# Four-layer sequence kernel: attention output transfers on GpSimd's queue, the first batch's split parts stored once, the first fills issued from two queues

## The reference

```python
c6 = silu(c) @ Wc + bc
sh_msa, sc_msa, g_msa, sh_mlp, sc_mlp, g_mlp = split(c6, 6)
xm = modulate(layernorm(x), sh_msa, sc_msa)
q, k, v = heads(xm @ Wq + bq) / 16, heads(xm @ Wk + bk), heads(xm @ Wv + bv)
w = softmax(q @ k.T, axis=-1)
x = x + g_msa * (merge(w @ v) @ Wo + bo)
x = x + g_mlp * (gelu(modulate(layernorm(x), sh_mlp, sc_mlp) @ W1 + b1) @ W2 + b2)
```

## Time and profile before

| | us |
|---|---|
| median of 3 runs (lowest, highest) | 965.06 (964.97, 965.78) |
| the profiled execution | 965.65 |
| its span in the trace | 963.8 |
| PE busy in the span | 899.0 (93%) |
| DVE, ACT, POOL busy | 585.8, 521.3, 417.0 |

### The profile page before, as it was taken

How to read it: one execution, slowest core, us unless ns; L and a number is a source line. 1 busy time by engine, 2 the same in 40 slices (tenths; PEclk the granted TensorE clock), 3 DMA queues, 4 the chain that set the end, 5 groups by cost and what they waited for, 6 DMA issues and landing times.

```text
span 963.8 us, 14588 instructions
## 1 busy us (share of the span) xinstructions
PE 899.0 (93%) x5256; PEld 539.6 (56%) x5256; DVE 585.8 (61%) x914; ACT 521.3 (54%) x952; POOL 417.0 (43%) x556
## 2 busy tenths in 40 slices
PE   5779999899899989998999998999999999999997
PEld 3444344334336778787788675343443433588874
DVE  4657877588975375556433178678778886234423
ACT  2118777476766445345265432567677776744431
POOL 4333152242648546347634434762441015575331
PEclk9979999799999999999999999999999999999999
DMA  7466656455310230014025125565464421100001
GB/s 221 118 192 219 206 153 172 140 138 159 92 46 33 81 129 1 23 56 158 1 93 200 12 79 158 160 190 168 131 196 134 112 80 47 46 13 1 23 22 44
DMA packets 67151, 102.33 MB, mean 106 GB/s; under 512 B 16540, under 2 KB 27880, under 8 KB 66696
## 3 DMA queue, kind: packets, MB, share of 16 engines
q1 hardware_dynamic: 63876, 97.50, 33.6%
q10 hardware_dynamic: 3204, 3.90, 1.3%
HBM read 64.65 MB, written 36.07 MB: 104 GB/s over the span
## 4 chain that ended last, share of the span: by engine, by line
PE 72%; DVE 8%; ACT 5%; issue 4%; DMA 4%; POOL 3%; SPq 3%; ACTq 0%; DVEq 0%; POOLq 0%
PE PS L1048 12%; PE PS L666 12%; PE PS L636 12%; PE PS L1030 11%; PE PS L593 6%; PE PS L584 6%; PE PS L645 3%; ACT PH L727 3%; DVE U L823 2%; PE PS L430 2%; DMA d_parts<-UR 2%; PE PS L604 2%; PE PS L1163 1%; PE PS L1151 1%; POOL PHR L1095 1%
## 5 line engine op out<-in xcount | busy, mean ns | idle before, releaser
L823 DVE TENSOR_REDUCE U<-PS 128x2 f32<-128x1024 f32 x256 | 308.4, 1219 | 70.9 <-PE PS L645 69.7
L727 ACT ACTIVATE PH<-PS 128x512 f32<-128x512 f32 x512 | 277.6, 598 | 103.3 <-PE PS L636 99.9
L636 PE MATMUL PS<-UR 50*128 50x512 f32 x512 | 197.1, 456 | 11.2 <-ACT PH L727 5.9
L645 PE MATMUL PS<-UR 48*128 48x512 f32 x512 | 193.8, 473 | 12.9 <-DMA UR<-d_parts 6.6
L1095 POOL TENSOR_TENSOR PHR<-PH,PHR 128x512 fp32r<-128x512 f32 x96 | 128.8, 1346 | 118.2 <-ACT PHR L1085 118.2
L636 PEld LDWEIGHTS PS<-UR 50*128 50x128 f32 x512 | 83.0, 188 | 167.8 <-ACT PH L727 107.1
L1048 PE MATMUL PS<-UR,PHR 128*128 128x256 f32 x768 | 159.9, 291 | 4.8 <-POOL PHR L1095 3.6
L666 PE MATMUL PS<-PH,U 128*32 128x512 f32 x1024 | 138.7, 614 | 0.0
L1048 PEld LDWEIGHTS PS<-UR,PHR 128*128 128x128 f32 x768 | 125.5, 190 | 22.5 <-issue 15.7
L1048 PE MATMUL PS<-W2R,PHR 128*128 128x256 f32 x384 | 108.7, 283 | 0.0
L1084 ACT ACTIVATE PH<-PS,col 128x512 f32<-128x512 f32 x64 | 44.0, 687 | 99.8 <-PE PS L1030 99.8
(11 more groups left out here) (238 smaller groups left out, 1248.7 us busy)
## 6 DMA issues: line engine op xcount, KB each, us to landing
UR<-d_parts SPq DMA_DIRECT2D x128, 192.0 KB, 4.1
d_parts<-UR SPq DMA_DIRECT2D x78, 256.0 KB
d_o<-U SPq DMA_DIRECT2D x32, 256.0 KB, 2.2
U<-in_L_cond_W_dram SPq DMA_DIRECT2D x8, 1024.0 KB, 7.9
W<-in_L_cond_W_dram SPq DMA_DIRECT2D x24, 256.0 KB, 2.9
U<-d_o SPq DMA_DIRECT2D x32, 128.0 KB
U<-d_rec SPq DMA_DIRECT2D x16, 256.0 KB
gates<-d_gate SPq DMA_DIRECT2D x3, 1024.0 KB, 5.2
```

Source lines behind the costliest of these rows:

```text
L636: self.close(pe.matmul(dst, KP[g // 2][r:r + SROWS + 2, j, kt * P:(kt + 1) * P], QP[g // 2][r:r + SROWS + 2, j, :], start=True, stop=True) ...
L645: ins = pe.matmul(bank(2 + (w + 2) % 4), QP[g // 2][r:r + SROWS, j, qt * P:(qt + 1) * P], KP[g // 2][r:r + SROWS, j, :], start=True, stop= ...
L727: nc.scalar.activation(PH[:, m % 2, j, :], self.where("ST", n), ACT.Exp).then_inc(self.a_free, 1)
L823: v.tensor_reduce(mx[:, G % 2, :].rearrange("p (r c) -> p r c", r=2)[:, :, c // 2], PS[:, 2 + (w + 1) % 4:4 + (w + 1) % 4, :], AX.X, ALU.m ...
```

## The change

For batch 0 of the first attention the high part is stored once (two transfers a save) and each fill reads it twice, so a fill has eight transfers instead of four. The K part of fill 0 is issued by ACT, that of fill 1 by POOL, which also issues the saves of half 1; both were SP's or ACT's. POOL normalizes two tiles of batch 0 and DVE the other two. OLOAD, RSAVE and RLOAD of the first seven pairs of both attentions go from SP to POOL's queue, and the steps of RCP, RSAVE, RLOAD and NORM move back by 4 to 7. Two groups of small loads (LDS 1 and 2, eight transfers) move to the front of SP's list. Semaphores are regrouped to fit; that part of the diff is left out here.

```diff
--- before.py
+++ after.py
 FILLS = 4 * 16
 LEAD, TAIL = -34, NSTEP + 4
 SLOTS = {"Q": (0, 0, 1), "K": (0, 1, 0)}
+FIRST_SLOTS = {"Q": ((0, 1, 0), (0, 2, 1)), "K": ((0, 2, 0), (0, 1, 2))}
...
         if G % 2:
-            put(16 * G + 38, "RCP", G // 2, 0)
-            put(16 * G + 39, "RSAVE", G // 2, 0)
-            put(16 * G + 46, "RLOAD", G // 2, 0)
-            put(16 * G + 56, "NORM", G // 2, 0)
+            put(16 * G + (45 if G < NG - 1 else 38), "RCP", G // 2, 0)
+            put(16 * G + 46, "RSAVE", G // 2, 0)
+            put(16 * G + 52, "RLOAD", G // 2, 0)
+            put(16 * G + 60, "NORM", G // 2, 0)
     for i in range(8):
         put(22 + 16 * i, "LDW", i, 0)
     if not rope:
         for i in range(3):
-            put(54 + 16 * i, "LDS", i, 0)
+            put((54, -95, -95)[i], "LDS", i, 0)
...
-        def rstd(pool, link, k):
+        def rstd(pool, link, k, done=None):
...
-            link(pool.tensor_tensor(rs[:, 2, :], rs[:, 0, :], rs[:, 1, :], ALU.mult))
+            ins = pool.tensor_tensor(rs[:, 2, :], rs[:, 0, :], rs[:, 1, :], ALU.mult)
+            if done is None:
+                link(ins)
+            else:
+                ins.then_inc(done, 1)
+                pool.wait_ge(done, 1)
 
         def norm_pool(pool, link, k, b, waits):
 
-            rstd(pool, link, k)
+            if k == 1:
+                pool.wait_ge(first_half, 1)
+            rstd(pool, link, k, None if k else first_rs)
             for s, n in waits:
                 pool.wait_ge(s, n)
-            for t in range(TT):
+            for t in range(TT if k else TT // 2):
                 ins = pool.tensor_scalar(xnorm[:, t, :], x[:, TT * b + t, :], rs[:, 3, t:t + 1], rs[:, 2, t:t + 1],
                                          ALU.add, ALU.mult)
             ins.then_inc(ln_done, 1)
+
+        def norm_first_half(v):
+            v.wait_ge(first_rs, 1)
+            for t in range(TT // 2, TT):
+                ins = v.tensor_scalar(xnorm[:, t, :], x[:, t, :], rs[:, 3, t:t + 1], rs[:, 2, t:t + 1],
+                                      ALU.add, ALU.mult)
+            ins.then_inc(first_half, 1)
...
                         pe.wait_ge(ln_done, self.norm0 + b + 1)
+                        if self.a == 0 and b == 0:
+                            pe.wait_ge(first_half, 1)
...
-                            pe.wait_ge(self.filled[g], FILLS * (self.b0 + b + 1))
+                            pe.wait_ge(self.filled[g], self.parts_filled(b, g))
+                            if self.first(b) and g == 1:
+                                pe.wait_ge(first_filled, FILLS)
...
-                    if kind == "WK" and self.a == 0 and b == 0:
-                        if i == 1:
-                            act.wait_ge(self.filled[0], FILLS)
-                            self.save_parts(act, "WQ", b, i)
+                    if self.first(b) and (kind, i) == ("WK", 0):
                         self.save_parts(act, kind, b, i)
+                    elif self.first(b) and (kind, i) == ("FILL", 0):
+                        self.fill(act, b, i, "K")
...
+                    elif kind in ("OLOAD", "RSAVE", "RLOAD") and not self.last_pair(kind, b):
+                        self.output_task(pool, kind, b)
+                    elif self.first(b) and (kind, i) == ("FILL", 1):
+                        pool.wait_ge(self.filled[0], self.parts_filled(0, 0))
+                        self.save_parts(pool, "WQ", b, 1)
+                        self.save_parts(pool, "WK", b, 1)
+                        self.fill(pool, b, i, "K")
...
-                        pool.wait_ge(self.oloaded[b % 2], 32 * (self.b0 + b // 2 + 1))
-                        pool.wait_ge(self.rloaded[b % 2], 16 * (self.b0 + b // 2 + 1))
+                        pool.wait_ge(*self.output_loaded(b))
...
             def save_parts(self, eng, kind, b, i, quarter=0):
                 k = kind == "WK"
                 eng.wait_ge(self.split[i], 2 * b + k + 1)
                 p = slice(64 * quarter, 64 * quarter + 64) if (b, i) == (0, 0) else slice(0, P)
-                for slot, c in enumerate(SLOTS[kind[1]]):
+                for slot, c in enumerate((0, 1) if self.first(b) else SLOTS[kind[1]]):
                     eng.dma_start(d_parts[self.a, 4 * b + 2 * i + k, slot][:, p.start // HD:p.stop // HD].rearrange(
-                        "d h t -> h d t"), parts_d[2 * i + k][p, c, :]).then_inc(self.saved[i], 16)
-
-            def fill(self, sp, b, g):
-                sp.wait_ge(self.saved[g // 2], self.parts_saved(g // 2, b, int(b > 0 or g > 0)))
+                        "d h t -> h d t"), parts_d[2 * i + k][p, c, :]).then_inc(
+                            first_saved if self.first(b) and i else self.saved[i], 16)
+
+            def fill(self, eng, b, g, kinds="QK"):
+                eng.wait_ge(*self.parts_saved(g // 2, b, int(b > 0 or g > 0)))
                 if b:
-                    sp.wait_ge(self.a_full, self.scored(64 * (b - 1) + 16 * g + 15))
-                for k, dst in enumerate((QD[g // 2], KD[g // 2])):
-                    src = d_parts[self.a, 4 * b + 2 * (g // 2) + k].rearrange("s d h t -> (s d) h t")
+                    eng.wait_ge(self.a_full, self.scored(64 * (b - 1) + 16 * g + 15))
+                for c in kinds:
+                    k, dst = int(c == "K"), (QD if c == "Q" else KD)[g // 2]
+                    src = d_parts[self.a, 4 * b + 2 * (g // 2) + k]
+                    done = first_filled if self.first(b) and (c, g) == ("K", 1) else self.filled[g]
                     for r in range(2):
-                        sp.dma_start(dst[64 * r:64 * r + SROWS, 2 * (g % 2):2 * (g % 2) + 2, :],
-                                     src[:, 4 * (g % 2) + r:4 * (g % 2) + 4:2, :]).then_inc(self.filled[g], 16)
+                        for s0, s1, at_ in FIRST_SLOTS[c] if self.first(b) else ((0, 3, 0),):
+                            r0 = 64 * r + HD * at_
+                            eng.dma_start(dst[r0:r0 + HD * (s1 - s0), 2 * (g % 2):2 * (g % 2) + 2, :],
+                                          src[s0:s1].rearrange("s d h t -> (s d) h t")[
+                                              :, 4 * (g % 2) + r:4 * (g % 2) + 4:2, :]).then_inc(done, 16)
+
+            def parts_filled(self, b, g):
+                return FILLS * (self.b0 + b + 1) + (FILLS if g != 1 else 0)
...
+            def last_pair(self, kind, b):
+                return (b // 2 if kind == "OLOAD" else b) == NG // 2 - 1
...
+            def output_task(self, eng, kind, b):
+                hp = b // 2 if kind == "OLOAD" else b
+                loaded, sums = self.output_loaded(hp)[0], self.sums_loaded(hp)[0]
+                if kind == "OLOAD":
+                    eng.wait_ge(self.osaved[b % 2], 16 * (2 * self.b0 + b // 2 + 1))
+                    if hp >= 2:
+                        eng.wait_ge(self.y, hp - 1)
+                    src = d_o[self.a, b].rearrange("(j r) t -> j r t", j=4)
+                    r0 = 64 * (b % 2)
+                    eng.dma_start(Onum[hp % 2][r0:r0 + 64, :], src[:, 0:HD, :]).then_inc(loaded, 16)
+                    eng.dma_start(Osum[hp % 2][r0:r0 + 64, :], src[:, HD, :].rearrange(
+                        "j (a c) -> j a c", c=32)).then_inc(sums, 16)
+                elif kind == "RSAVE":
+                    eng.wait_ge(self.rec, NG // 2 * self.a + hp + 1)
+                    eng.dma_start(d_rec[self.a, hp].rearrange("j (a c) -> (j a) c", c=32),
+                                  Osum[hp % 2]).then_inc(self.recips_saved(hp)[0], 16)
+                elif kind == "RLOAD":
+                    eng.wait_ge(*self.recips_saved(hp))
+                    eng.dma_start(Oden[hp % 2], d_rec[self.a, hp].unsqueeze(1).to_broadcast([8, HD, T])).then_inc(
+                        loaded, 16)
...
-                        self.fill(sp, b, i)
+                        self.fill(sp, b, i, "Q" if self.first(b) and i < 2 else "QK")
...
-                    elif kind == "OLOAD":
-                        sp.wait_ge(self.osaved[b % 2], 16 * (2 * self.b0 + b // 2 + 1))
-                        hp = b // 2
-                        if hp >= 2:
-                            sp.wait_ge(self.y, hp - 1)
-                        src = d_o[self.a, b].rearrange("(j r) t -> j r t", j=4)
-                        r0 = 64 * (b % 2)
-                        sp.dma_start(Onum[hp % 2][r0:r0 + 64, :], src[:, 0:HD, :]).then_inc(self.oloaded[hp % 2], 16)
-                        sp.dma_start(Osum[hp % 2][r0:r0 + 64, :], src[:, HD, :].rearrange(
-                            "j (a c) -> j a c", c=32)).then_inc(self.sloaded[hp % 2], 16)
-                    elif kind == "RSAVE":
-                        sp.wait_ge(self.rec, b + 1)
-                        sp.dma_start(d_rec[self.a, b].rearrange("j (a c) -> (j a) c", c=32),
-                                     Osum[b % 2]).then_inc(self.rsaved[b % 2], 16)
-                    elif kind == "RLOAD":
```

(39 more changed lines are left out.)

12 lines of the change are left out of this document (7 added, 5 removed).

## The result

The changed kernel takes 962.81 us (median of 20 runs, 957.64 to 966.22) and the kernel before, beside it, 967.78 us. The ratio is 0.9938, 95% interval 0.9919 to 0.9957: faster by 0.6%, about 6 us, where 952 with a range of 944 to 961 stood. The profiled execution took 958.8 us (span 957.0), 6.85 less than that of before, and is among the quickest three of the 20; what follows is counted against it.

The account below looks back on a forecast made before the run. TensorE, busy 93% of the span, was taken as the bound. Terms -7.5 - 9.6 + 3.1 + 1 + 0.3 = -12.7, and 0.6 from profile to median, took 965.65 to 952 us, range 944 to 961.

Parts of the forecast that it names:

- number 6: Output tasks waiting on GpSimd: nothing in steady state, +3.1 us and +1 for the clock at first MLP, +0.3 at second.
- the start: First fills up to step 16 of the first attention: -7.5 us, bounds -12.1 and -3.
- the middle: TensorE's stop before step 112 of the first attention, a wait for maxima plus half clock: gone, -9.6 us.
- Point 1: First normalization shared between GpSimd and VectorE, two tiles each: 0.7 us earlier, nothing if they hinder each other.
- Point 2: High parts stored once, fewer save bytes: first fill issued at 30.2, landed at 35.2, 3.7 us earlier.
- Point 3: Second-half saves and fill 1's keys on GpSimd: step 0 at 60, SyncE's maxima setting step 16 at 78.9, not 86.4.
- Point 4: Eight small second-layer loads moved to SyncE's idle time before its first save: nothing gained.
- Point 5: Output loads, reciprocal saves and loads moved to GpSimd: SyncE's maxima 3.5 us earlier, mid-attention stop gone, -9.6 us.
- A: Rival: a stop moves instead of going, by half clock at step 16 or mid-attention; 957 to 962 us, chance 0.18.
- B: Rival: only the bytes help, fill 1 hanging on DMA engines; start -3.7, total 956; chance 0.66 together with the forecast.
- C: Rival: GpSimd's DMA issues are dear, delaying the key fill and MLP starts; mostly above 965 us, chance 0.08.
- a sign of error: Listed as showing the forecast wrong: among others, TensorE waiting for y before PJ; no size given.

Follow-up runs that it names:

- experiment 1: The changed kernel with both state-space chains on GpSimd moved early, to steps 4 and 40; 949.69 us, ratio 0.9829 to the kernel before.
- experiment 2: The changed kernel with only the first state-space chain moved early, to step 40, the second staying at step 190; 955.36 us, ratio 0.989.
- experiment 8: The changed kernel, chains early and pair 6's reciprocals on SyncE, with first-batch parts stored three times again; lead at step 0 fell to 1.1 us, no run time given.
- experiment 6: The changed kernel with the eight small loads back at steps 70 and 86; median above the 957 to 963 us expected, exact time not given.
- Experiment 9: The changed kernel, chains early and pair 6's reciprocals on SyncE, with the second half's four saves back on ScalarE; 9.2 us of lead lost between steps 0 and 32.
- experiments 4 and 5: First: kernel before with eight small loads moved early, median 9.2 us under it. Second: changed kernel, output tasks on SyncE, small loads at old steps; time not given.
- experiment 7: The changed kernel with both chains early, plus pair 6's reciprocal save and load on SyncE in both attentions; 948.3 us, ratio 0.9815.
- numbers 7 and 12: The same kernel run twice: changed kernel, chains early, pair 6's reciprocals on SyncE; 948.3 us (0.9815), then on another run 951.48 us (0.9837).

## Why the prediction was wrong

**The step that failed is number 6,** "In the steady state there is room". It looked at GpSimd's idle time ahead of a projection's add in the second attention, where no state-space chain runs, and took the schedule's step numbers for RLOAD and NORM (+52, +60) as the times at which they run. On an in-order queue a step number only gives a place. In the first attention S5N stands between RSAVE and RLOAD for pair 3 (158, 162, 164) and pair 4 (190, 190, 196), 12 us each, longer than the whole way from RSAVE to PJ allows. Cost: 4.65 + 3.65 = 8.3 us for 0; experiment 1 gives them back, experiment 2 the first alone. With 8.3 off, the changed kernel's profile would stand at 950.5 (the forecast's sum for a profile is 953); experiment 1's is at 950.1, with 1.3 us more at step 16, which its edit does not explain, and 1.3 more lost in the first MLPs. By parts the profile has -7.5 at the start, -9.2 in the middle, +8.3 here, +1.0 in the first MLPs, and +2.3 and -1.5 in the second attention, -6.6 of the 6.85 measured.

- Point 1 (0.7 us): right. Both halves take 1.12 us side by side, done at 13.91.
- Point 2 (first fill issued at 30.2, landed at 35.2): issued at 31.16, used at 37.98. Its term was too small, though: it counted the bytes only for the first fill; experiment 8 shows 8.2 us at step 0. The share of DMA engines while the first saves run is 0.26 as before, at 89 GB/s. From the first fill's use to the key fill's issue it took 42.53 - 37.98 = 4.6 us against 5.8 planned, and the cheaper issue alone accounts for it (4 x 0.34 = 1.4). So GpSimd's saves gave no sign of landing 2 or 3 us sooner, as I had worked out by the rule of the next engines in the Trainium skill (DMA: Bandwidth & Descriptors, "Why a DMA increments its semaphore by 16 and not by 1").
- Point 3: step 0 at 63.33 (60), maxima at 72.44 (71), the start -7.5 (-7.5). The total was right by luck, for two errors cancel: step 0 came 3.3 us late, and TensorE's wait at step 16 was 0.86 us (78.77) and not 4.6. The second fill landed at 51, not 48, for GpSimd had to wait longer for the first one, and its issue cost 0.53 to 0.66 us and not 1.0. That SyncE sets step 16 held here, but by little: with the same start experiments 1, 2 and 6 show no wait for the maxima there. That ScalarE's issues hold TensorE up held for before: there TensorE waits 3.19 us at 50.47 for a projection's eviction (L707) that stands behind them, and the changed kernel has no such wait. Experiment 9 does not bring it back, for its saves go out earlier; it loses by later landings.
- Point 4, the small loads at nothing: mis-sized. They are 3.3 us of SyncE's queue ahead of the critical maxima, and their place decides the whole stop, 9.2 us, in the kernel before and with the changed start (experiments 4 and 5). I had written "up to 8 x 0.6 us off SP ahead of the critical maxima" and priced it at 0, since point 5 had spent the gain already.
- Point 5: -9.6, measured -9.2, but mostly by another cause. Moving the output tasks speeds the maxima by 1.7 to 2.0 us, not 3.5; that takes the stop away where the loads stay (experiment 6), but here the loads had done so. Its own balance here is a loss: with the output tasks on SyncE the rest of the change takes 951.8 us (ratio 0.9863), with them on GpSimd 962.8 (0.9938), and the intervals do not touch.
- Point 6, the first MLP +3.1, and +1 for the clock: 2.4 at the first low part, 1.0 left later; 2.6 by experiment 7. The second MLP +0.3: nothing, the leads at step 255 and at the end agree to 0.1.
- Not in the forecast: 2.3 us at the start of the second attention, in which the change has no part (next section but one).

Of the rivals, A's time (957 to 962) is the nearest to the median of 962.8, but not its cause: the maxima of step 16 brought no half clock, and the stop in the middle went. B (956) put the start at -3.7, and it gave 7.5. C fell: no issue of GpSimd's took over 0.86 us, and the 84 of the output took 0.58 to 0.74. The wait for a VectorE operation that the Trainium skill (SBUF — State Buffer, its box on the "DVE blocks DMA" trap) describes would show as an issue longer by up to 1.2 us, and none is; but VectorE's long operations here read PSUM, so this is no test of that rule. What was listed as a sign of error, TensorE waiting for y before PJ, is what came.

## What to carry to other kernels

Before a task moves to another engine's in-order queue, list what stands ahead of each of its instances there, not only how busy the engine is: a long block without a deadline (here 12 us of scalar arithmetic) belongs where the queue would idle and its inputs are there, ahead of the tasks with deadlines. And price the edits of a bundle one by one against the same stop: what two of them remove is gained once, and here the one that cost nothing would have done.

## What the hardware showed beyond that

The clock did not answer in the same way to the same wait. At the start of the second attention TensorE waits 1.86 us for ScalarE's XN in every profile, at the same place of the program. In before the granted clock stays 1.00 there; in the changed kernel it is at half for several us (windows of the changed kernel, the wait ending at 603.21):

```profile
600.00:604.00 4.00, 2.14 (x11) 1.33 (x9) 2.45 (x2) 3.52 (x5) 3.76 (x3) 0.84 0.52 202
604.00:608.00 4.00, 4.00 (x8) 1.36 (x7) 0.00 (x0) 0.98 (x2) 0.00 (x0) 0.50 0.53 204
```

Steps 0 to 8 took 9.1 us in six of the 14 profiles of this study and 11.4 us or more in the other eight. In four of the eight a stretch of half clock came some 10 us before that wait as well, so there what TensorE had done before was not quite the same. At step 16 of the first attention, waits of up to 1.25 us for the maxima left the clock alone, and after waits of 1.86, 2.04 and 2.97 us it was at half for 6.8 to 13.7 us; with the wait, 5.0, 6.7 and 9.2 us were lost from step 0 to step 32. At step 228 waits of 1.48 to 1.70 us (changed kernel, experiments 2 and 6) brought 3.4 us of half clock each. What decides between the two outcomes of a wait of the same length, these runs don't show. The Trainium skill (TensorE: Matmul & The Clock Gate, "Part 1: The HAM clock gate") says that the chip's watch on TensorE's activity does not start with the kernel, so that the same kernel meets it differently from run to run; the 14 profiles agree with that and do not prove it. It would explain a part at least of the spread of 944 to 955 us among the runs of number 7's kernel (numbers 7 and 12), whose fastest run has a mean granted clock of 0.987 and whose slowest 0.976. In these profiles a stop of 2 us cost anything from 2 to 7.
